# Where the value products stand among the score units of an attention stage

## The reference

```python
x = x + _layernorm(_L0_attn_ref(_layernorm(x), W_q, W_k, W_v, W_o))
x = x + _layernorm(_L0_ffn_ref(_layernorm(x), gate_w, gate_bias, Wg, Wu, Wd, Ws_g, Ws_u, Ws_d))
# attention, 16 heads of 16 channels, rotary Q and K
score = jnp.einsum('bnqd,bnkd->bnqk', Q, K) / jnp.sqrt(jnp.float32(D_K))
attn = softmax(where(causal, -inf, score))
out = jnp.einsum('bnqk,bnkd->bnqd', attn, V)
# experts: 4 of 16 for each token, and a shared one
y = jnp.einsum('nei,ne,ehi->nh', silu(hg) * hu, cw, Wd) + shared
```

## The kernel before

| third | T1 and T2 | S1 | S2 | AV |
|---|---|---|---|---|
| 0 | 256 | 512 | 384 + 128 | 384 + 128 |
| 1 | 512 | 256 | 512 | 256 |
| 2 | 384 + 128 | 384 + 128 | 256 | 512 |

## Time and profile before

### The profile page before, as it was taken

How to read it: one execution, slowest core, us unless ns; L and a number is a source line. 1 busy time by engine, 2 the same in 40 slices (tenths; PEclk the granted TensorE clock), 3 DMA queues, 4 the chain that set the end, 5 groups by cost and what they waited for, 6 DMA issues and landing times.

```text
span 1094.3 us, 22252 instructions
## 1 busy us (share of the span) xinstructions
PE 890.9 (81%) x7190; PEld 660.5 (60%) x7190; DVE 679.7 (62%) x1941; ACT 463.7 (42%) x788; POOL 452.6 (41%) x424
## 2 busy tenths in 40 slices
PE   4359798898998998896897898799999988899660
PEld 3236465665665565564565555587877876788550
DVE  4466657768678678777575585764643355573853
ACT  2114454544453444443444545455444544355330
POOL 4321203117306306404322315457567645565560
PEclk9669989897798699898788789899999998899885
DMA  3675865236335435533658312366567798757943
GB/s 136 153 193 119 222 158 130 74 77 175 96 79 153 118 84 128 145 83 82 180 154 286 104 43 96 116 184 197 175 189 211 207 357 274 254 168 234 331 181 144
DMA packets 108654, 177.51 MB, mean 162 GB/s; under 512 B 15232, under 2 KB 79744, under 8 KB 108288
## 3 DMA queue, kind: packets, MB, share of 16 engines
q1 hardware_dynamic: 93952, 135.45, 44.3%
q0 software_dynamic: 14592, 40.65, 9.9%
HBM read 92.35 MB, written 83.17 MB: 160 GB/s over the span
## 4 chain that ended last, share of the span: by engine, by line
PE 48%; DVE 18%; issue 9%; SPq 9%; DMA 6%; POOL 5%; ACT 5%; POOLq 0%; DVEq 0%; ACTq 0%
PE ring L1396 7%; PE ring L1268 5%; PE ring L1202 5%; PE ring L1203 4%; PE ring L1204 4%; PE ring L1239 4%; DVE nmax L749 4%; PE ring L1254 4%; PE ring L1417 3%; POOL expert_rows L668 3%; SPq L571 3%; DMA xg<-sorted_rows 2%; PE ring L1216 2%; ACT prob L1132 2%; PE ring L1382 2%
## 5 line engine op out<-in xcount | busy, mean ns | idle before, releaser
L749 DVE TENSOR_REDUCE nmax<-ring 128x2 f32<-128x1024 f32 (+3 forms) x256 | 201.1, 818 | 90.4 <-PE ring L1245 88.5
L1132 ACT ACTIVATE prob<-ring 128x1024 f32<-128x1024 f32 (+1 forms) x192 | 164.7, 879 | 200.8 <-PE ring L1259 192.4
L668 POOL DMA_INDIRECT expert_rows<-ys,dest x176 | 183.1, 1040 | 109.8 <-ACT ys L1086 46.5
L1396 PE MATMUL ring<-we,xh 128*128 x704 | 174.9, 393 | 0.0
L660 POOL DMA_INDIRECT sorted_rows<-xr,idx_all x128 | 127.7, 998 | 83.6 <-DVE xr L908 50.4
L1396 PEld LDWEIGHTS ring<-we,xh 128*128 128x128 f32 x704 | 132.8, 199 | 15.5
L1239 PE MATMUL ring<-k_st,q_st 48*128 48x512 f32 (+3 forms) x512 | 112.5, 449 | 35.4 <-ACT prob L1132 28.6
L1254 PE MATMUL ring<-q_st,k_st 50*128 50x384 f32 (+3 forms) x512 | 107.0, 437 | 35.1 <-DMA q_st<-mrow 17.0
L970 DVE SCALAR_TENSOR_TENSOR sl<-sl,got,ring 128x128 f32<-128x128 f32 x176 | 53.1, 344 | 114.6 <-ACT sl L1184 113.2
L1268 PE MATMUL ring<-prob,v_sb 128*32 128x512 f32 (+3 forms) x1024 | 110.5, 535 | 0.8 <-ACT prob L1132 0.4
L638 POOL TENSOR_TENSOR rot<-rot 128x512 f32<-128x512 f32 x16 | 20.4, 1274 | 218.7 <-DVE rot L741 218.7
(11 more groups left out here) (189 smaller groups left out, 1639.6 us busy)
## 6 DMA issues: line engine op xcount, KB each, us to landing
xg<-sorted_rows SPq DMA_DIRECT2D x176, 134.0 KB
parts<-part SPq DMA_DIRECT2D x32, 512.0 KB
ykt<-expert_rows SPq DMA_DIRECT2D x8, 2048.0 KB, 10.3
k_st<-parts SPq DMA_DIRECT2D x64, 128.0 KB
q_st<-parts SPq DMA_DIRECT2D x64, 128.0 KB
sorted_rows<-zeros SPq DMA_DIRECT2D x3, 2144.0 KB, 9.9
sorted_rows<-zeros SPq DMA_DIRECT2D x48, 134.0 KB, 2.3
we<-w_exp SPq DMA_DIRECT2D x1, 6144.0 KB, 20.3
```

The costliest lines, as they stand in the source:

```text
L668: pool.indirect_dma_start(out=yk, out_offset=bass.IndirectOffsetOnAxis(ap=dest[:, j % 8, b:b + 1], axis=0), in_=ys[:, j % NYS, b, :], in_o ...
L749: dve.tensor_reduce(nmax[:, Q % 2, :, pp, qb], slot[:, :, col:col + (qb + 1) * P], AX.X, ALU.max, negate=True).then_inc(s_max, 1)
L1132: act_e.activation(prob[:, u % 2, 2 * half:2 * half + 2, 0:width], slot[:, :, 0:width], ACT.Exp, scale=SCALE).then_inc(s_exp, 1)
L1396: last = pe.matmul(G_BANK[j % 2][:, b, :], xh[:, j % 2, b, k, :], we_cols[:, bass.ds(columns[j, b] + k * D, D)], start=(k == 0), stop=(k = ...
```

## The change

The time of each AV goes from 1.4 to 1.15 past its ST. In a third it now stands behind S1 and ahead of T2, where it stood behind S2 and ahead of the fillers.

```diff
         for m in range(UNITS):
-            add(3 * Q + 7 + m + 1.4, "AV", Q, m)
+            add(3 * Q + 7 + m + 1.15, "AV", Q, m)
```

## The result

The changed kernel takes 1090.63 us (median of 4, 1084.49 to 1096.57) against 1105.61 before, a ratio of 0.9883 with a 95% interval of 0.9838 to 0.9928. Over its 16 executions of the three the mean is 1093.5 us, 11 less than that of the kernel before; the forecast was 16.5 less.

What follows compares the result with a forecast made beforehand. Mostly PE sets the time, DVE around the layer norm. Filled waits sum to 8.7 + 5.1 + 0.8 + 4.3 - 1.6 - 0.8 = 16.5 us, so 1105.6 becomes 1089.1; own range 1076 to 1099, 8 in 10 for 1066 to 1107.

Steps and rivals of the forecast that it cites:

- Third 2 behind the router ... Together 8.7 us: S2 waits for ACT's exponential after a table load, six times in the trace; AV fills these waits, 8.7 us faster.
- DVE was idle in the waits at the router: Argument against no change: DVE was busy 8.16 of 10.20 us in the stretch at the router.
- Left are 5.1: S2's waits for exponentials of size 512, 6.2 us in all, 1.1 of it not counted: 5.1 us faster.
- the `h_lo` and `z` waits of third 1: ST's waits at T2: three for `h_lo` give 1.2 us, the two for `z` 1.1 us.
- So these four give nothing: Third 0, four of six `xt_lo` waits: CNT still waits for `att` behind S2's maximum on DVE; no gain.
- as a whole minus 0.8: Sum for thirds 0: 0.8 us gained for `xt_lo`, minus 1.6 for CNT, so 0.8 us slower.
- The rest lies inside DVE's stretch: Long waits in the layer norm's third 2: filling them gives nothing, as PE then waits longer before HT.
- the wait before HT: PE's wait before the transposes HT was to grow by 2 us or so in each sequence.
- That S1 waits newly: S1 of third 0 waits newly for T2's exponential, about 0.35 us twice and 0.1 once: minus 0.8 us.
- the one with no change: Rival, chance 0.20: DVE's order binds in more places, 8.7 and 5.1 are given back before HT; 2.7 faster, 1103 us.
- The clock before HT: Rival, slower, chance 0.10: PE idles 5 us before HT and the clock falls, costing 5 us each in five sequences; 1114 us.
- The clock behind the router: Rival, chance 0.18: AV fills the idle time, the clock stays full, up to 27 us more; below 1076 us.

Runs made afterwards that it cites:

- the two later ones: The changed kernel without further edit, compared again with the kernel before: 1094.74 us, ratio 0.9894, and 1093.96 us, ratio 0.9898.
- only thirds 2: AV moved between S1 and T2 in thirds 2 only, against the kernel before: 1098.08 us, ratio 0.9915.
- The router's AV alone: AV moved only in the third 2 behind the router, 8 of 96, against the kernel before on a slower chip: 1149.01 against 1160.64 us, ratio 0.9894.
- only thirds 1: AV moved between S1 and T2 in thirds 1 only, against the kernel before: 1099.16 us, ratio 0.9935.
- By itself third 0: AV moved in thirds 0 only, against the kernel before, in two calls: 1098.62 us, ratio 0.9886, and 1099.70 us, ratio 0.9947.
- thirds 1 and 2: AV moved in all but thirds 0, against the kernel before: 1140.90 us, ratio 0.9841 (slower chip), and 1090.08 us, ratio 0.9857.
- one place further ahead: AV between T1 and S1 in every third, against the kernel before on the slower chip: 1167.25 against 1160.64 us, ratio 1.0056.

## Why the prediction was right, and where its parts were not

The time was right (1090.6 for 1089), and so was the main mechanism: AV goes into the waits at S2 and T2, and the exponential waits fall. That the time is so close is in part luck: the first comparison has 15 us by the medians, the two later ones 9 and 11, and the 16 executions together 11, where the sum was 16.5. Its terms fared unequally.

"Third 2 behind the router ... Together 8.7 us" was mis-sized. The waits were filled, but LG to CNT got only some 0.4 us shorter instead of 1.7: the first four sequences have a mean of 32.4 us before and 32.0 in the three traces of the changed kernel. That goes in one of two ways. Where the clock is up, PE waits again, 1.71 and 0.83 us, for DVE, whose queue holds the routing steps there. Where it is at half for longer, PE waits nowhere but works longer: by windows, the two sequences that begin at 284.5 and 366.2 of the changed kernel:

```profile
284.50:316.90 32.40, 28.10 (x307) 19.85 (x308) 22.37 (x63) 14.43 (x21) 7.49 (x8) 0.89 0.32 91
366.20:398.40 32.20, 30.72 (x306) 21.48 (x307) 22.35 (x63) 14.27 (x21) 7.44 (x7) 0.79 0.32 92
```

Both take about the same; ten of the twelve are within 0.3 us of them, the shortest is 30.3. My argument against it ("DVE was idle in the waits at the router") looked at the first 10 us alone. What only thirds 2 gained came with the clock. The router's AV alone gave 9.3 us, of which 1 to 5 are left at equal clock.

"Left are 5.1" and the `h_lo` and `z` waits of third 1 held together: 6.8 us at equal clock for 7.4. In the trace of only thirds 1 no wait for `prob` is left at size 512 and the three short ones for `h_lo` are gone, but the two long ones grew from 1.76 to 2.3 us each and `z` is waited for 1.7 us in all, 1.8 before. So the time fits and not each part of it.

"So these four give nothing" for third 0, as a whole minus 0.8: the order on DVE was right (CNT's wait 1.42, forecast 1.6; the wait for `xt_lo` gone). The price was wrong, since it counted the wait alone. The longer wait is mostly followed by half clock, 3.4 or 6.8 us of it, and third 0 likely costs the whole change some 5 us, all of them with the clock. By itself third 0 gains 6, at equal clock 8 to 9. No sum of waits gives both. They are measured, and the second is not explained.

"The rest lies inside DVE's stretch" held: LN to HT is 18.6 us in the first three sequences of the changed kernel and 18.6 to 18.7 before. But the wait before HT didn't grow by 2 us; for `nmax` at L1216 it is 2.5 us in all after and 4.0 before, and T1 waits for a maximum instead. That S1 waits newly held in size, 0.31 to 0.54 us, but five times, 2.3 us for the 0.8 of the sum.

Of the rivals, the one with no change had its mechanism right for the router, and it took most of that term. The clock before HT did not get worse (HT to LG 85 to 86 us over the seven sequences, 91 before). The clock behind the router did not stay up: in the first four sequences it is at half for 3.4 to 13.7 us there, mostly 13.7, where it was 6.8 and three times 10.2. The Trainium skill, "TensorE: Matmul & The Clock Gate", section "A second HAM failure mode: psum-queue depth-cycling", says that frequent micro-idles make the clock swing; by that, filling them should have freed the clock as well. The runs agree in part: the mean clock is 0.871 for 0.867, in only thirds 2 it is 0.881 and in thirds 1 and 2 0.879, but in thirds 0 or 1 alone it is no higher; and the whole change was not worth more than its waits. Open stays why a third moved alone and the three together differ: 7.3, 4.8 and 5.8 us by the means, 18 in sum, and 11 together.

## What to carry to other kernels

Work that is ready early can be put between a slot's producer and the next user of that slot (here 1% faster; one place further ahead it was 0.6% slower than before), but what that frees is worth only what the following stretch can take: ask which engine's queue sets the end of the next 20 us, not whether it idled at the wait. Price a move by every stage of the period and let each place have its own order: here thirds 1 and 2 are likely better without third 0. And compare medians of many executions with their clocks before two traces, and all sequences of a trace before one.

## What the runs showed of the hardware

Executions of one kernel on one chip differed by 14 us (1097.78 to 1111.83) and followed the mean granted clock, 6.9 us for 0.01 there and 6.2 with the executions of another chip. A third chip took 5% longer for the same kernel (1160.64 for 1103.81 us). A wait of 1.42 us before CNT was followed by half clock within some 2 us 15 times of 18, one of 0.81 with no idle time at S2 behind it in none of 12. A stretch took about the same time at 0.89 and at 0.79 of the clock, 32.4 and 32.2 us; at the higher clock PE waited for DVE (1.71 and 0.83 us).
